# A new order for the first stage of an eight-block transformer on one core, and the fp8 sum ahead of the head maxima in its last attention

## The reference

```python
# layer 0, both blocks on a layer norm of x
v = jnp.einsum('bsd,hd->bsh', visual_features, Wv) + bv
t = jnp.einsum('bsd,hd->bsh', text_features, Wt) + bt
dots = jnp.einsum('bih,bjh->bij', v, t)
out = dots / jnp.maximum(vn[:, :, None] * tn[:, None, :], EPS)      # norms of v and t: a cosine
...
logits = xf @ gate_w.T
w, sel = jax.lax.top_k(logits, 2);  w = softmax(w)
expert_out = jnp.einsum('nc,edc->ned', xf, expert_w)                # eight experts
# layer 1: the kernel of a state-space (S4D) convolution
powers = jnp.exp(dtA[:, :, None] * jnp.arange(L))
K = 2.0 * jnp.einsum('dn,dnl->dl', dC, powers).real
# end of layer 2, then layer 3
x = x + jnp.tanh(g_ffn[2]) * fake_quant_fp8_linear(x)
attn = softmax(einsum('bihd,bjhd->bhij', q, k) * SCALE)             # eight heads of 64
```

## Time and profile before

| | |
|---|---|
| timed runs (3) | median 1556.45 us, 1553.75 to 1558.42 |
| profiled execution | 1556.44 us, span 1554.5 us, mean granted TensorE clock 0.842 |
| busy, share of the span | PE 77%, DVE 65%, ACT 44%, POOL 38% |
| first stage | 0 to 218.4 us |
| L3 attention, main part | 1020 to 1264 us: PE busy 223.4 us of 244, DVE 154.9, ACT 150.4, POOL 85.4 |

### The profile page before, as it was taken

The page is one execution under the profiler, slowest core; times in us unless marked ns, Lnnn a source line. Parts: engine busy times, 40 slices in busy tenths (PEclk is TensorE's granted clock), DMA queues, the critical chain, the costliest instruction groups (busy, mean ns, idle before and its releaser), DMA issues. The chain is left out here.

```text
span 1554.5 us, 30934 instructions
## 1 busy us (share of the span) xinstructions
PE 1201.6 (77%) x10597; PEld 813.4 (52%) x10597; DVE 1010.5 (65%) x3921; ACT 685.5 (44%) x1990; POOL 585.7 (38%) x792
## 2 busy tenths in 40 slices
PE   3676743676666678884799897489999969999997
PEld 3443322343443445553577676146666647777765
DVE  6876649999994379852577776557766544444432
ACT  3343335556565344320344443146666633433332
POOL 3466665888876155421222321223333310000000
PEclk8588865666667789996899999589999979898988
DMA  6310041000000511000000000000000000000001
GB/s 164 83 41 1 0 106 26 15 18 28 25 22 28 150 41 42 15 14 14 2 3 3 3 3 3 1 1 1 2 1 2 1 1 1 0 0 0 0 0 54
DMA packets 63678, 35.54 MB, mean 23 GB/s; under 512 B 23925, under 2 KB 61424, under 8 KB 63538
## 3 DMA queue, kind: packets, MB, share of 16 engines
q1 hardware_dynamic: 62234, 33.45, 8.0%
q10 hardware_dynamic: 1304, 0.33, 0.1%
HBM read 25.21 MB, written 6.42 MB: 20 GB/s over the span
## 5 line engine op out<-in xcount | busy, mean ns | idle before, releaser
L2774 DVE SCALAR_TENSOR_TENSOR k_X<-ps,m_gt,k_X 128x128 f32 (+1 forms) x256 | 72.1, 344 | 125.4 <-PE ps L2673 125.4
L2703 ACT ACTIVATE m_hid<-ps,k_b 128x512 f32<-128x512 f32 x128 | 81.8, 684 | 137.5 <-PE ps L2673 127.7
L2673 PEld LDWEIGHTS ps<-k_w,m_hid 128*128 128x128 f32 x1024 | 123.1, 192 | 26.8 <-issue 17.2
L2664 PE MATMUL ps<-m_xnT,k_w 128*128 128x512 f32 x256 | 130.5, 641 | 1.1 <-DVE m_lg L2719 1.1
L2673 PE MATMUL ps<-k_w,m_hid 128*128 128x128 f32 x1024 | 123.4, 275 | 0.0
L2380 POOL TENSOR_TENSOR l_p<-l_p,l_rsum 128x512 f32<-128x512 f32 x64 | 65.2, 1039 | 152.5 <-DVE l_rsum L2611 152.5
L2182 DVE TENSOR_REDUCE g_top<-ps 128x8 f32<-128x1024 f32 x64 | 75.4, 1220 | 50.5 <-PE ps L2050 50.5
L1447 DVE MATCH_REPLACE8 c_left<-c_top,c_left 128x128 f32<-128x128 f32 x384 | 100.9, 276 | 0.0
L2492 ACT ACTIVATE l_p<-ps,l_shift 128x128 f32<-128x128 f32 x256 | 91.3, 387 | 20.2 <-DVE l_shift L2549 20.2
L2130 ACT ACTIVATE g_pT<-ps 128x1024 f32<-128x1024 f32 x64 | 62.0, 1021 | 85.4 <-PE ps L2066 85.4
L692 PE MATMUL ps<-f_expT,f_xeT 128*128 128x512 f32 x128 | 71.0, 686 | 33.6 <-DVE k_X L1064 33.6
(11 more groups left out here) (515 smaller groups left out, 3250.2 us busy)
## 6 DMA issues: line engine op xcount, KB each, us to landing
v_toep<-kpad SPq DMA_DIRECT2D x4, 1024.0 KB, 10.4
fo_dram<-c_fo SPq DMA_DIRECT2D x32, 128.0 KB, 1.7
v_late<-kpad SPq DMA_DIRECT2D x4, 1024.0 KB, 10.5
d_fo<-fo_dram SPq DMA_DIRECT2D x8, 512.0 KB, 3.5
k_X<-in_x SPq DMA_DIRECT2D x8, 256.0 KB, 3.5
out<-k_X SPq DMA_DIRECT2D x4, 512.0 KB, 5.4
f_cx<-in_ctx SPq DMA_DIRECT2D x4, 384.0 KB, 5.3
c_cx<-in_ctx SPq DMA_DIRECT2D x4, 384.0 KB, 3.6
```

Of the source, the lines that this page charges most:

```text
L2664: pe.matmul(ps[:, 4 * u + q, :], k.w1_3[:, e, 128 * q:128 * q + 128], xnT[:, u], start=True, stop=True).then_inc(s["hid_ps"].sem, 1)
L2673: m = pe.matmul(ps[:, 4 * u + 2 + e % 2, j * S:j * S + S], hid[:, u, q, j * S:j * S + S], k.w2_3[:, e, q, :], start=q == 0, stop=q == 1)
L2703: act.activation(hid[:, u, q, :], ps[:, 4 * u + q, :], ACT.Gelu, bias=k.b1_3[:, 2 * e + q:2 * e + q + 1]).then_inc(s["hid"].sem, 1)
L2774: dve.scalar_tensor_tensor(out=xj[u][j], in0=ps[:, 4 * u + 2 + e % 2, j * S:j * S + S], scalar=gt[:, u, j, e:e + 1], in1=xj[u][j], op0=ALU ...
```

## The change

It moves instructions on four engines in the first stage, and two on DVE in the L3 attention. No computation of the reference changes.

First stage, by engine:

- **DVE.** The two halves of `c_add` go from the end of a step into the next one, between its expert batches 0, 1 and 2; `e_stats`, `e_apply`, `c_stats` and `c_most` follow one batch each. The power products are spread differently: `angles` stands ahead of the second group's statistics, the powers up to 4 are made in steps 0 and 1, those up to 8 at the ends of steps 1 and 2, and those up to 16 at the end of step 3, where `xp_done` now stands (it stood at the end of step 2). The one-column product for the 16th power and its `factor` are gone.
- **POOL.** New `sixteenth` (ten instructions: two complex squarings of the fourth power) at the end of step 1. `e_power` and `c_power` stand after other gathers: `c_power` of the next group comes after `c_inverse`, not before it. `coefficients_a` goes behind the first inverse.
- **PE.** Three expert batches, not two, stand ahead of `c_turn`; the turns of the gating stand around `c_norms`, in step 1 the gates ahead of the norms. The kernel sum goes from behind the last eight batches to ahead of them.
- **ACT.** The weights' copies stand ahead of `er`, the sine behind the first projection copies, `c_apply` behind batch 6, with `e_exp` between its halves from step 2 on; the copies for the film and the kernel stand among the last batches.

```diff
+            def square(a, b, c, d, e):
+                tt_(c, a, a, ALU.mult)
+                tt_(e, b, b, ALU.mult)
+                tt_(c, c, e, ALU.subtract)
+                tt_(d, a, b, ALU.mult)
+                link(pool.tensor_scalar(d, d, 2.0, None, ALU.mult))
+
+            def sixteenth():
+                pool.wait_ge(w_done, 3)
+                square(wr[:, 2, :], wi[:, 2, :], r[5], r[6], r[7])
+                square(r[5], r[6], w16r, w16i, r[7])
...
                 for i in range(PAIR):
                     if 0 <= s - 2 < TURNS:
                         gather((s - 2) * PAIR + i)
-                    if i == 1 and 2 <= s + 1 < TURNS:
-                        c_power(s + 1)
+                    if i == 2 and 0 <= s - 1 < TURNS:
+                        e_power(s - 1)
+                    if i == 3 and s == 1:
+                        coefficients_c()
                     if i == 4 and s < TURNS:
                         c_inverse(s)
+                    if i == 5 and 2 <= s + 1 < TURNS:
+                        c_power(s + 1)
...
+                if main:
+                    experts(b0 + 6)
+                if 2 <= s + 1 < TURNS:
+                    c_apply(s + 1, 0)
+                    c_apply(s + 1, 2)
+                if 1 <= s - 1 < TURNS:
+                    e_exp(s - 1)
...
                 if s == 2:
-                    powers_im(8, 3)
-                    factor(16, 4)
+                    powers_im(4, 2)
+                    factor(8, 3)
+                if s == 3:
+                    powers_re(8, 3)
                     dve.sem_inc(xp_done, 1)
...
+                g = due(n, 10)
+                if g is not None:
+                    dve.wait_ge(o8_ps, g + 1)
+                    dve.wait_ge(xb8_done, g + 1)
+                    dve.scalar_tensor_tensor(out=group(g), in0=ps[:, 7, :].rearrange("p (j d) -> p j d", j=G),
+                                             scalar=k.unscale[:, 0:1], in1=group(g), op0=ALU.mult,
+                                             op1=ALU.add).then_inc(x8_done, 1)
                 if 0 <= n + 1 < B:
...
-                    dve.tensor_scalar(shift[:, a, :], top[:, a, :], -SCALE, None, ALU.mult).then_inc(shift_done, 1)
-                g = due(n, 10)
-                if g is not None:
-                    dve.wait_ge(o8_ps, g + 1)
-                    dve.wait_ge(xb8_done, g + 1)
-                    dve.scalar_tensor_tensor(out=group(g), in0=ps[:, 7, :].rearrange("p (j d) -> p j d", j=G),
-                                             scalar=k.unscale[:, 0:1], in1=group(g), op0=ALU.mult,
-                                             op1=ALU.add).then_inc(x8_done, 1)
+                    if i == 0:
+                        dve.wait_ge(minus_done, 1)
+                    dve.tensor_tensor(shift[:, a, :], top[:, a, :], minus[:], ALU.mult).then_inc(shift_done, 1)
```

More of the change, by code:

```diff
@@ L709, in _ @@
                 b0 = (s - 2) * PAIR
+                if main:
+                    experts(b0)
+                    experts(b0 + 1)
+                    experts(b0 + 2)
                 if s == 4:
@@ L731, in _ @@
                 if main:
-                    experts(b0 + 2)
-                if 0 <= s - 1 < TURNS and main:
-                    e_turn(s - 1, 0)
+                    experts(b0 + 3)
                 if s < TURNS:
@@ L737, in _ @@
                 if main:
-                    experts(b0 + 3)
+                    experts(b0 + 4)
                 if 0 <= s - 1 < TURNS:
-                    if not main:
-                        e_turn(s - 1, 0)
+                    e_turn(s - 1, 0)
+                if s < TURNS and main:
+                    c_norms(s)
+                if 0 <= s - 1 < TURNS:
                     e_turn(s - 1, 1)
                 if main:
-                    experts(b0 + 4)
-                if s < TURNS:
-                    c_norms(s)
+                    experts(b0 + 5)
                 if 0 <= s - 1 < TURNS:
@@ L755, in _ @@
                     experts(b0 + 7)
-                if s == 5:
+                if s == 4:
+                    pe.wait_ge(copied, 2)
+                    pe.matmul(ps[0:C, 2, :], wv1T[:], wfilm[:].rearrange("p a n -> p (a n)"), start=True,
+                              stop=True).then_inc(film_ps, 1)
+                    for h in range(2):
+                        m = pe.matmul(ps[:, 3, 128 * h:128 * h + 128], wd2T[:, h, :], wd2T[:, h, :], start=True, stop=True)
+                    m.then_inc(gram_ps, 1)
+                if s == 4:
                     pe.wait_ge(u_done, 1)
@@ L841, in _ @@
                     experts(b0)
-                    experts(b0 + 1)
+                if s == 5:
+                    act.wait_ge(gram_ps, 1)
+                    act.wait_ge(dcoef_done, 1)
+                    for h, g0 in ((0, 0), (1, 129)):
+                        for e in range(4):
+                            p = slice(32 * e, 32 * e + 32)
+                            act.activation(k.dcoef[p, h, g0 + 32 * e:g0 + 32 * e + 32],
+                                           ps[p, 3, 128 * h + 32 * e:128 * h + 32 * e + 32], ACT.Identity)
@@ L888, in _ @@
                     act.activation(k.tmask[:], ps[:, 0, 128:128 + B], ACT.Identity)
+                if s == 0:
+                    act.wait_ge(exp_ps, 1)
+                    for h in range(2):
+                        act.activation(expT[:, 4 * h:4 * h + 4, :].rearrange("p e d -> p (e d)"), ps[:, 6 + h, :],
+                                       ACT.Identity).then_inc(exp_done, 1)
                 if s == 5:
```

175 lines of the change are left out of this document (75 added, 100 removed).

## The result

The changed kernel takes 1546.79 us (median of 5, 1542.28 to 1548.84) against 1556.45 for the kernel before (1553.75 to 1558.42). The ratio is 0.9930, 95% interval 0.9914 to 0.9946, so it is faster by 0.5 to 0.9%. The forecast was 1534. It lies 12.8 us too low, and the measured time is just inside its range (1547). The profiled execution took 1542.8 us, at the fast end of the five.

The account below looks back on a forecast made before the run. No engine was full in the first stage, where a circular chain set the step; PE bound the L3 attention. 1556.4 minus 12.7 (first stage) minus 10.1 (L3) gave 1533.6, taken as 1534 us, range 1521 to 1547.

Parts of the forecast that it names:

- (a): First stage's opening: turned weights no longer wait on ACT, sine moved later; first group summed 6.5 us earlier, 34.5 for 41.
- (b): Step 1 of the first stage: first expert on DVE at 60.4, second group's statistics done at 71.5, before 73.3.
- (c): Steps 2 and 3, first stage: ends at 97 and 131, waits 0.8 us (root) and 3 us (`e_exp`), 12 us ahead.
- (d): Step 4, first stage: new mask wait of 5 us, half hidden by late POOL; ends at 167 against 185.
- (e): First stage's last step: chain 4.8 us, sum 4.5 us ahead of the experts; stage ends 205.7 against 218.4, 12.7 gained.
- (f): L3 attention: fp8 sum ahead of the maximum removes PE's waits; 10.1 us gained, bounds 2 and 14.
- The term for the clock: L3 attention: PE's clock fell behind two waits, 1.7 us lost in each; 2.4 of 3.4 us counted as regained.
- The first, POOL as the new bound: First stage: DVE and POOL block each other, 9.6 us over 32 batches, stage gains only 3; 1543 us, chance 0.14.
- The others: L3 order fails, 1542 us, chance 0.09; more than forecast, 1526, 0.11; slower by TensorE's clock, up to 1585, 0.04.
- TensorE's half clock: First stage: TensorE falls to 1.2 GHz in stalls and stays, 1.6 us lost per batch; up to 1585 us, chance 0.04.

Follow-up runs that it names:

- u_skip_rows: Changed kernel with POOL's chain end behind batch 20's gather, skip additions behind batch 27's, mask load on its own semaphore, late rows behind group 3's roots; 1525.47 us.
- chain_out: Changed kernel without POOL's product chain, a memset standing in for its output (wrong numbers in the kernel sum); 1533.57 us, ratio 0.9850.
- norms_later: Changed kernel with TensorE's norms and dots of the next group, and VectorE's read of them, behind a step's sixth batch; 1544.38 us, ratio 0.9936.
- mask_apart: Changed kernel with the mask load on its own semaphore, waited for only ahead of the mask's conversion; 1544.86 us, ratio 0.9944.
- u_early: Changed kernel with the last part of POOL's product chain moved from behind step 4's gathers to behind batch 20's gather; 1534.18 us, ratio 0.9874.
- l3_alone: Kernel before with only the L3 part of the change (fp8 sum ahead of the maxima, shift by tensor_tensor); 1543.12 us, ratio 0.9938.
- front_alone: Changed kernel's first block with the L3 block of the kernel before; 1555.92 us, ratio 1.0010.
- sum_behind: Changed kernel with the kernel sum and ScalarE's four copies of it put back behind the last eight batches; 1533.88 us, ratio 0.9866.

## Why the forecast was right in L3 and wrong in front

The forecast's landmarks of the first block, in us:

| landmark | before | forecast | changed |
|---|---|---|---|
| first group summed | 41 | 34.5 | 34.1 |
| first expert on DVE | 73.3 | 60.4 | 60.2 |
| statistics of group 1 done | 73.3 | 71.5 | 72.5 |
| step 2 ends | 109 | 97 | 101.4 |
| step 3 ends (before its cosine sum) | - | 131 | 138.2 |
| wait for the mask | - | 5 | 4.5 |
| step 4 ends | 185 | 167 | 177.3 |
| chain done, sum begins | - | 170 | 181.5 |
| batch 24 | 189.0 | 175.5 | 188.1 |
| last batch done | 203.7 | 191.8 | 204.9 |
| next stage | 218.4 | 205.7 | 219.2 |

**(a), (b)** were right within 1 us: PE's first turn at 11.5 us, the group summed at 34.1, the first expert at 60.2.

**(c) is the step that failed first: the lengths of steps 2 and 3.** Step 2 ends 4.4 us late, of which 1.0 stood at its start (72.5 for 71.5) and 3.4 arose in it; step 3 took 36.9 us for 34, 2.9 more. The two waits that it named were smaller (0.4 us for 0.8 for the root, 1.1 for 3 for `e_exp`). But it put DVE's waits for PE at nothing, and PE let DVE wait 2.6 and 1.0 us in step 2, 0.4, 4.6 and 1.4 in step 3. TensorE's clock goes with 1.7 us of step 2 (28.7 against 27.0) and 1.5 of step 3 (36.9 against 35.4, both against u_skip_rows). The chain beside the powers has 0.6, by chain_out. The last 2.5 us stay open: they belong to PE's row of turn, norms, experts and gates, or to DVE's own work, and norms_later shows only that the place of the norms in that row isn't it, since the waits come back elsewhere.

**(d) failed next: the length of step 4**, 39.0 us for 36. The mask's wait was right, 4.5 for 5. What it had wrong was POOL. It let half of the wait be hidden by a POOL that is late by 3 to 4 us; mask_apart shows all of it hidden, by a POOL that would be 5.7 us late. Without POOL's chain (chain_out) step 4 takes 36.4 us, the mask's wait included, so POOL's products ahead of it account for 2.6 of the 3.0 us. In u_skip_rows, with the mask apart and the late rows moved, it takes 33.3.

**(e)** was right in kind and short by 2.3 us. It priced the chain at 4.8 us (4.9 measured) and the sum at 4.5 (4.4), and had itself charged 8.5 us between DVE's end of step 4 and batch 24; it was 10.8. The chain began 0.8 us ahead of DVE's end, not 2, behind POOL's last gather of step 4, and the first experts behind the sum took 2.2 us (185.9 to 188.1), not 1. So of the 13.5 us by which the next stage came later than forecast, 10.3 stood at the end of step 4, 2.3 came ahead of batch 24, and 0.9 behind it.

What (e) didn't see is that most of its own charge could be avoided, and this is why the new order gave nothing against the old one. u_early changes only when the chain is done, 167.7 for 181.4. Its DVE is where the changed kernel's is at the end of step 4 (late work done at 176.9 against 177.3), and yet batch 24 comes at 179.5 instead of 188.1 and the next stage at 209.5 instead of 219.2. Those 8.6 to 9.7 us are what a better place of the chain is worth. They are not the size of the forecast's error, which had booked 8.5 of them as a cost.

**(f)** held: 11.4 us for 10.1 (by the length of L3 it is 9.6 in l3_alone against the kernel before, and 9.9 between the changed kernel and front_alone). The five waits are gone, the wait for the turned copies grew by 1.2 us in all, where 0.5 in each case was forecast, and the shift is as long as it was. The term for the clock, 1.7 us in each of two cases, has no row: the earlier trace rows show 0.9 us (1.92 for 1.02). In the trace all 64 products of that line (now L2469) together took 33.8 us instead of 35.0.

**The rivals.** The first, POOL as the new bound, had 0.14 and 1543 us, and its outcome is what came. POOL bounds step 4 (mask_apart, chain_out) and the start of the last step (u_early); that it bounds steps 2 and 3 is not shown. The argument against it, that POOL has 17 us of room in step 1, was no argument for steps 3 to 5, where the chain now stood. Its own price (one blocked product a batch, 9.6 us) is not what cost: DVE's blocked powers and factors have 0.6 us of step 2. The others did not come. TensorE's half clock went with 1.5 to 1.7 us in a step of the changed kernel, in other traces with up to 4.2, not with 1.6 a batch. That the forecast's 1534 equals sum_behind and u_early (1533.9 and 1534.2) is luck: their steps are as long as the changed kernel's, and a shorter way to batch 24, with what L3 and the later stages gave over the forecast, makes up for it.

## What to carry to other kernels

A step in which no engine is full has to be laid out with every engine's row, the one that feeds the busiest engine too. Here the forecast named DVE's waits for POOL and ACT, put those for PE at nothing, and steps 2 to 4 came out 9.3 us longer.

When work is moved ahead of a queue, ask when its last input is ready on the engine that makes it, and whether that engine can make it sooner. Here 4.9 us of products behind POOL's gathers, and the sum behind them, undid nearly all of the 8.0 us that the steps had won, and moving the products ahead of three gathers brought 8.6 to 9.7 us back. Where a wait is removed and nothing is gained (the mask), read what ends the next wait on that engine at the same time; the bound was another queue. A move ahead should also take along what stands behind it: the store that the early sum had made free to go stayed last, at 6.4 us.

## What the runs showed of the hardware

TensorE's clock in one and the same place differs from run to run. Sixteen one-column products of the norms took 1.06 us in nine traces and 1.87 in three, with the granted clock at 0.82 to 1.00 and at 0.69 to 0.75. The level of 1.2 GHz follows short waits of PE (0.65 and 1.31 us ahead of the norms in the changed kernel, 0.64 and 1.30 in u_skip_rows), but nearly the same waits left the second at full clock, so a forecast of one step can't be better than some 2 us here.

DVE beside POOL: the last two of the four factor copies (`tensor_scalar` and copy, 64x128), in the changed kernel with POOL's chain running and then in chain_out without it:

```profile
99.47 0.70 DVE L965 TENSOR_SCALAR f_wi<-f_YP 64x128 f32<-64x128 f32 x1
100.21 0.57 DVE L966 COPY f_wi<-k_x 64x128 f32<-64x128 f32 x1
```

```profile
98.37 0.27 DVE L963 TENSOR_SCALAR f_wi<-f_YP 64x128 f32<-64x128 f32 x1
98.67 0.27 DVE L964 COPY f_wi<-k_x 64x128 f32<-64x128 f32 x1
```

This is 0.70 and 0.57 us against 0.27 and 0.27. POOL pays in its turn: the addition of batch 30 took 2.38 us instead of 0.45 beside DVE's conversion of the mask, which ran from 204.88. The Trainium skill ("SBUF — State Buffer", section "Who interferes with whom") says that copies and `tensor_scalar` can take the port pair which DVE shares with GpSimd, and that whoever comes second is blocked; the trace agrees in both directions.

The kernel sum's 128 products (256 matmuls in the trace) stop once, for 1.9 to 2.7 us, with no releaser, as they did before, wherever the sum stands. One thing in the traces goes with it. In all sixteen, one transfer of 16 KB on the queue that the profile calls instruction (q8) begins within 0.5 us of the stop, and the matmuls go on 1.2 to 1.4 us behind its end, after a short stop as after a long one: in the changed kernel it ends at 183.9 and they go on at 185.2, in sum_behind at 196.0 and 197.5. That the stop waits for this transfer fits all of them; no run moved it, so it is not shown.
